# Second attention layer: the value products of four of twelve key tiles as three rounded passes

## The reference

```python
q = (hidden_states @ Wq).reshape(B, Sq, H, D)          # 16 heads of 128
k = (encoder_hidden_states @ Wk).reshape(B, Skv, H, D)
v = (encoder_hidden_states @ Wv).reshape(B, Skv, H, D)
q = rmsnorm(q, gq)
k = rmsnorm(k, gk)
scores = jnp.einsum('bqhd,bkhd->bhqk', q, k) * scale
attn = jax.nn.softmax(scores, axis=-1)
out = jnp.einsum('bhqk,bkhd->bqhd', attn, v)
return out.reshape(B, Sq, H * D) @ Wo
```

## Time and profile before

| | |
|---|---|
| median of 3 runs | 2175.83 us (2175.75 to 2176.48) |
| the profiled execution | 2174.4 us, its span 2172.6 us |
| TensorE busy | 2110.9 us (97%) |
| VectorE busy | 1575.4 us (73%) |
| GpSimd busy | 1409.9 us (65%) |
| ScalarE busy | 972.9 us (45%) |
| mean granted clock of TensorE | 0.998 |

### The profile page before, as it was taken

How to read it: one execution, slowest core, us unless ns; L and a number is a source line. 1 busy time by engine, 2 the same in 40 slices (tenths; PEclk the granted TensorE clock), 3 DMA queues, 4 the chain that set the end, 5 groups by cost and what they waited for, 6 DMA issues and landing times. The chain is left out here.

```text
span 2172.6 us, 27566 instructions
## 1 busy us (share of the span) xinstructions
PE 2110.9 (97%) x8962; PEld 1571.2 (72%) x8962; DVE 1575.4 (73%) x2592; ACT 972.9 (45%) x2593; POOL 1409.9 (65%) x1120
## 2 busy tenths in 40 slices
PE   7999999999999999999999988999999999999999
PEld 7777777777777777777777556666666666665998
DVE  4889888898889888988896642556665666652677
ACT  3444445545454445444545337544444344431432
POOL 1468776887778777877787237187878787771221
PEclk9999999999999999999999999999999999999999
DMA  3000000000000000000001410011011111101110
GB/s 132 29 15 16 29 29 15 21 23 29 15 29 15 29 19 25 15 29 29 15 10 40 140 46 1 29 43 57 29 57 30 56 49 37 43 1 52 37 52 25
DMA packets 15136, 75.63 MB, mean 35 GB/s; under 512 B 1746, under 2 KB 2114, under 8 KB 13986
## 3 DMA queue, kind: packets, MB, share of 16 engines
q1 hardware_dynamic: 14994, 73.89, 10.4%
HBM read 72.97 MB, written 0.92 MB: 34 GB/s over the span
## 5 line engine op out<-in xcount | busy, mean ns | idle before, releaser
L612 POOL TENSOR_TENSOR l_prod<-l_prod 125x256 f32<-125x256 f32 x576 | 417.4, 738 | 270.4 <-DVE l_prod L677 269.7
L677 DVE TENSOR_TENSOR l_prod<-l_side,xq 125x512 f32<-125x512 f32 x576 | 394.9, 686 | 56.2 <-PE l_side L809 48.3
L954 POOL TENSOR_TENSOR l_acc<-l_acc,l_probs 125x896 f32<-125x896 f32 x160 | 346.0, 2162 | 81.7 <-ACT l_probs L904 66.0
L553 ACT ACTIVATE l_probs<-l_slots,mask_bias 125x448 f32<-125x448 f32 x384 | 237.8, 632 | 340.6 <-PE l_slots L748 340.5
L974 DVE TENSOR_TENSOR l_scaled<-l_slots,rk 125x896 f32<-125x896 f32 x192 | 207.0, 1085 | 197.8 <-PE l_slots L1039 197.7
L606 POOL TENSOR_TENSOR l_acc<-l_acc,l_probs 125x896 f32<-125x896 f32 x160 | 338.6, 2116 | 0.0
L535 ACT ACTIVATE l_prod_act<-l_prod_act 125x128 f32<-125x128 f32 x768 | 228.0, 298 | 235.3 <-DVE l_prod_act L677 235.3
L904 ACT ACTIVATE l_probs<-l_scaled 125x896 f32<-125x896 f32 x192 | 182.8, 952 | 320.7 <-DVE l_scaled L974 296.8
L686 DVE TENSOR_REDUCE l_msq<-l_prod 125x4 f32<-125x256 f32 x576 | 235.0, 410 | 1.7
L640 DVE SCALAR_TENSOR_TENSOR top<-l_side,mask_bias,top 125x448 f32<-125x448 f32 x330 | 223.4, 677 | 6.8 <-PE l_side L792 5.8
L1037 PE MATMUL l_slots<-l_qhi,l_clo 128*125 128x448 f32 x384 | 203.0, 529 | 1.4 <-DVE l_qlo L979 1.4
(11 more groups left out here) (258 smaller groups left out, 4487.9 us busy)
## 6 DMA issues: line engine op xcount, KB each, us to landing
land<-in_ctxT SPq DMA_DIRECT2D x32, 750.0 KB, 4.3
l_nat<-in_ctxN SPq DMA_DIRECT2D x16, 750.0 KB
post_we<-in_experts SPq DMA_DIRECT2D x20, 384.0 KB, 3.0
spare<-in_ctxN SPq DMA_DIRECT2D x8, 750.0 KB
nat<-in_ctxN SPq DMA_DIRECT2D x8, 750.0 KB
spare<-in_wo SPq DMA_DIRECT2D x2, 2048.0 KB, 8.5
spare<-in_wqT SPq DMA_DIRECT2D x4, 512.0 KB, 9.2
mid_fac<-in_factors SPq DMA_DIRECT2D x1, 2048.0 KB, 8.2
```

What stands on the lines that cost most here:

```text
L553: act.activation(P[t % NP][:, HALF * i:HALF * i + HALF], bank_of("S", t, i)[0:KT, 0:HALF], ACT.Exp, bias=m.mask_bias[:, b, t:t + 1]).then_ ...
L612: pool.tensor_tensor(buf[:, :, 0:C // 2], buf[:, :, 0:C // 2], buf[:, :, C // 2:C], ALU.add).then_inc(s.half_sum, 1)
L677: dve.tensor_tensor(to[:, :, :], bank, xt.unsqueeze(1).to_broadcast([KT, 4, C]), ALU.mult).then_inc(s.side_dve, 1)
L954: pool.tensor_tensor(acc[:, :], acc[:, :], P[t % NP][:, :], ALU.add).then_inc(s.acc, 1)
```

## The change

Tiles 2, 4, 6 and 8 of each batch (`SPLIT`) take the value product as three rounded passes instead of the full-precision product: both the natural-layout context (`nat`) and the probabilities (`P`) are split into a high part (a copy to float32r, on ScalarE) and a low part (the difference, on VectorE). The context's four tiles are split once for each batch, after step 10 of the batch before; the probabilities of each such tile on their own. The other eight tiles are as before.

```diff
+    SPLIT = [2, 4, 6, 8]
+    tiles_split = slice(2, 9, 2)
 ...
+        phi = [sb(f"phi{i}", [KT, QW], F32R) for i in range(2)]
+        plo = [sb(f"plo{i}", [KT, QW], F32R) for i in range(2)]
+        nat_hi = sb("nat_hi", [KT, len(SPLIT), C], F32R)
+        nat_lo = sb("nat_lo", [KT, len(SPLIT), C], F32R)
 ...  ScalarE
+            def probs_high(b, t):
+                at = SPLIT.index(t)
+                act.wait_ge(s.probs, NT * b + t + 1)
+                act.activation(phi[at % 2][:, :], P[t % NP][:, :], ACT.Copy).then_inc(s.p_hi, 1)
+            def values_high(b):
+                need(act, (s.ld_nat0, s.ld_nat1)[b % 2], 8 * (b + b % 2))
+                need(act, s.pv, NT * (b - 1) + SPLIT[-1] + 1 if b > 0 else 0)
+                act.activation(nat_hi[:, :, :], nat[b % 2][:, tiles_split, :], ACT.Copy).then_inc(s.nat_hi, 1)
 ...
                     for bt, tt in tile_ahead(LAG, b, t):
                         exp(bt, bt % 2, tt)
+                        if tt in SPLIT:
+                            probs_high(bt, tt)
+                    if t == SPLIT[-1] + 2 and nxt:
+                        values_high(b + 1)
 ...
             high_parts(0, 0)
+            values_high(0)
 ...  VectorE
+            def probs_low(b, t):
+                at = SPLIT.index(t)
+                dve.wait_ge(s.p_hi, len(SPLIT) * b + at + 1)
+                dve.tensor_tensor(plo[at % 2][:, :], P[t % NP][:, :], phi[at % 2][:, :].bitcast(F32), ALU.subtract).then_inc(s.p_lo, 1)
+            def values_low(b):
+                dve.wait_ge(s.nat_hi, b + 1)
+                dve.tensor_tensor(nat_lo[:, :, :], nat[b % 2][:, tiles_split, :], nat_hi[:, :, :].bitcast(F32),
+                                  ALU.subtract).then_inc(s.nat_lo, 1)
 ...
                     for bt, tt in tile_ahead(LAG, b, t):
                         scale_scores(bt, bt % 2, tt)
+                    if t + 1 in SPLIT:
+                        probs_low(b, t + 1)
+                    if t == SPLIT[-1] + 2 and nxt:
+                        values_low(b + 1)
                     if t == 0 and not start:
                         invert(b - 1)
 ...
             query_low(0, 0)
+            values_low(0)
 ...  TensorE, values_half
-                last = pe.matmul(psO[:, half, 0:HALF], nat[par][:, t, :], P[t % NP][:, cols], start=t == 0, stop=t == NT - 1)
+                if t in SPLIT:
+                    at = SPLIT.index(t)
+                    pe.wait_ge(s.nat_lo, b + 1)
+                    pe.wait_ge(s.p_lo, len(SPLIT) * b + at + 1)
+                    pe.matmul(psO[:, half, 0:HALF], nat_lo[:, at, :], phi[at % 2][:, cols], start=False, stop=False)
+                    pe.matmul(psO[:, half, 0:HALF], nat_hi[:, at, :], plo[at % 2][:, cols], start=False, stop=False)
+                    last = pe.matmul(psO[:, half, 0:HALF], nat_hi[:, at, :], phi[at % 2][:, cols], start=False, stop=False)
+                else:
+                    last = pe.matmul(psO[:, half, 0:HALF], nat[par][:, t, :], P[t % NP][:, cols], start=t == 0, stop=t == NT - 1)
```

More of the change, by code:

```diff
@@ L841, in second_attention @@
     s = semaphores(sem, tag, [
-        "ld_land", "ld_nat0", "ld_nat1", "ctx_hi", "ctx_lo", "q_hi", "q_lo", "scores", "scaled", "probs", "pv", "acc",
+        "ld_land", "ld_nat0", "ld_nat1", "ctx_hi", "ctx_lo", "q_hi", "q_lo", "scores", "scaled", "nat_hi", "nat_lo", "probs", "p_hi", "p_lo", "pv", "acc",
         "den", "inv", "o_raw", "o_done", "fold_pe", "fold_act", "fold_dve", "y_pe", "y_act"])
     LAG, NP = 2, 3
+    SPLIT = [2, 4, 6, 8]
+    tiles_split = slice(2, 9, 2)
     with ExitStack() as ctx:
```

## The result

The kernel after takes 2284.59 us (median of 4 runs, 2283.86 to 2285.12) against 2175.79 before: ratio 1.0501, 95% interval 1.0484 to 1.0517. Slower, as forecast, and 20 us over the 2265 predicted, inside the range of 2222 to 2300. The profiled execution has a span of 2283.2 us, 110.6 more than before.

A forecast was written before the change was run, and what follows sets the result against it. TensorE, without slack in `second_attention`, was taken to bound the kernel. Waits of 6.9 us less 1.1 saved, carried as +5.9 a batch, over fifteen batches 89 us, made 2174.4 into 2263, as a median 2265; range 2222 to 2300.

The forecast's parts named there:

- What comes off: TensorE's value products of four tiles in 16 batches: 0.28 us saved a tile, 17.9 us, called the whole gain.
- The walk: One batch followed through all engines' queues: 34.29 us becomes 40.2, +5.9 a batch, 89 us over fifteen batches.
- the faster rival: All engines in `second_attention`: everything added lies in slack, `probs_low(2)` is done by 8.2 us; 2158 us; chance 0.03.
- The port: VectorE and GpSimd exclude one another by whole instructions: a subtraction costs 1.09 us with GpSimd idle, up to 3.1 otherwise.
- Step 1, end of the batch before: Values of tile 0: TensorE waits 1.87 us for ScalarE's copy, as `values_low` waits for GpSimd's long instruction.
- Step 2, tile 2: Values of tile 2: TensorE waits 1.34 us for `probs_low(2)`, behind the reciprocals and scale 3 on VectorE.
- Step 3, tile 4: Values of tile 4: GpSimd's addition goes between the halves of `normalise`, `probs_low(4)` is late; TensorE waits 3.0 us.
- Step 4, tiles 6 and 8: Values of tiles 6 and 8: TensorE loses 0.04 and 0.66 us to `probs_low`; `query_low` delays the scale of tile 9.
- order at the port: VectorE's `normalise` keeps its second half ahead of GpSimd's addition; a batch is 2.0 us shorter, 2235 us; chance 0.20.
- the clock falls in the waits: TensorE's clock falls in tile 4's 3.0 us wait: 2.6 a batch, 39 more at most, up to 2304; chance 0.12.
- The first batch: No reciprocals or `normalise` ahead: some 0.5 us at tiles 4 and 8 against 0.28 saved each, about 0.
- Cheaper waits: Port costs less, `values_low` precedes GpSimd's long instruction: order alone, at least +1.3 a batch; 2195 to 2220; chance 0.07.

The follow-up runs named there:

- its twin with the clock kept up by force: The kernel after with 13 extra rounded passes on TensorE just before its wait for the low part of tile 4; 2265.61 us (1.041).
- The third experiment: The kernel after with `normalise` as one instruction of 896 columns in place of two of 448; 2238.31 us (1.0281).
- The splitting alone: The kernel after with TensorE taking all tiles in full precision, while the other engines still split; 2247.74 us (1.0329).
- the first experiment: The kernel after without splitting: TensorE's rounded passes for the four tiles take operands that are ready anyway; 2162.24 us (0.9935).

## Why the prediction held, and by what it was off

*What comes off,* 17.9 us: 13.6 measured with ready operands. The saving of tile 2 lies ahead of the one place where VectorE sets the time, which the first part of the prediction had named, and is absorbed there. The walk had that in it (it runs over VectorE's queue), the sum of "the whole gain" and the price of the faster rival, 2158, had not.

*The port,* "by whole instructions": right. `probs_low` took 1.07 at tile 2, where GpSimd is idle, and 2.09 at tile 4, as forecast; at tile 6, forecast at 2 or more, it took 1.08, since the addition was over by then.

*Step 1, end of the batch before,* 1.87: measured 1.79, from ready to start as the walk counts. *Step 2, tile 2,* 1.34: 1.22. *Step 3, tile 4,* 3.0: 2.94. *Step 4, tiles 6 and 8,* 0.04 and 0.66: 0 and 0.67. Each wait is where it was put, and the first pass after each takes 0.07 longer. That is 6.9 in all, as forecast, and less 1.1 and 0.1 it makes the 5.7 that a batch grew. The forecast's own terms make 5.7 too; the 5.9 that it carried on, to 40.2 a batch and 89 us, is 0.2 over their sum. The clock's price can be read between two rows above: 12.63 - 11.09 = 1.54 us. The batch in which the clock held is 40.02 against the walk's 40.2; its twin with the clock kept up by force 40.05.

*The rival "order at the port"* (0.20) fell. It was decided by one row of another kind of instruction, and that row was the right one: 3.07 for the two halves. The third experiment, in which the gap between them is taken away, ended at 2238 where that rival had put its own kernel at 2235.

*The rival "the clock falls in the waits"* (0.12) came true on top of the forecast, and this is the step that failed: the forecast had "a granted clock of 1.0" and put the clock at nothing. I read the earlier trace rows as if it took a wait of 3.39 us; a wait of 2.75 to 2.79 was enough in 12 of 13 batches. The trace of before has a second wait of that length, between the two layers, which the forecast doesn't use, and behind it the clock held (its row, and the stretch in the columns of the earlier trace rows):

```profile
1288.50 0.47 PE L1393 MATMUL mid_bk<-mid_sql,mid_one_r 128*128 128x448 f32 x1 [3.14 <-POOL mid_sql L1236]
...
1288.00:1292.00 4.00, 3.24 (x18) 2.58 (x18) 0.62 (x1) 1.54 (x4) 3.20 (x5) 1.00 0.00 0
```

With one fall and one hold at waits near the forecast's own 3.0, an even chance would have been right. Its size was off the other way: 1.5 in most batches, since only some nine passes ran slow, and 2.6 in the two where the clock stayed down twice as long.

*The first batch,* "about 0": its denominator comes at 1445.25 against 1442.81, 2.4 late. Its four split tiles wait 0.1, 0.3, 1.0 and 1.0 us from ready to start, the first pass after each takes 0.07 longer, and the stage starts 0.9 later (the term of 0 to 1), less 1.1 saved. "Some 0.5 us at tiles 4 and 8" was 0.3 and 1.0, and the 1.0 at tile 6 was left out.

The account of the span, all from the denominators: 14 batches at 40.02 - 34.34 = 5.7 are 79.5, and the last one 5.0 (38.68 against 33.64): 84.5, forecast 89. The first batch 2.4, forecast 0. All fifteen distances together grew by 106.7, 22.2 more. Of that 19.9 are the clock in 12 batches, forecast 0. The other 2.3 are the second batch (42.36), and not the fall at tile 4: with the passes put into that wait it is 42.32 all the same. Its wait at tile 0 is 3.85, as GpSimd's long instruction begins 1.4 us ahead of the denominator there and not 3.7, and the clock falls behind that wait in both kernels; what that fall costs isn't measured apart. Behind the last denominator 1.5. Sum 110.6. The last batch shows again that a fall can be free: the clock fell there behind a wait of 2.44, and it took 38.68 against 38.70 with the clock held.

*"Cheaper waits"* had its bound right though its case did not occur: at least 1.3 a batch by order alone, and 1.5 with the additions gone (with part of the wait behind the long instruction still in it).

What wasn't seen ahead is how the three engines' loop closes. I took the waits one by one, as delays of TensorE. The splitting alone costs 72 us with TensorE waiting for none of its results, and one wait taken away (`values_low` later) returned at the next tile. A walk finds the period because it carries all queues along; its single terms don't add up when one of them is removed.

## What to carry to other kernels

Where one engine is solid, as here, moving its work to engines with 70% busy time is priced not by their idle share but by the tightest spot in the period, here the two reciprocals, and by what shares a port with what: put a subtraction of two SBUF operands where GpSimd is idle, or let GpSimd's instruction wait for it. Two back-to-back VectorE instructions on SBUF leave GpSimd a gap to step into; one instruction doesn't. And a wait on TensorE that lies near one after which the clock has been seen to fall should be priced with the fall, unless another wait stands close behind it and takes the slow passes in.

## What the runs showed of the hardware that I had not expected

- A wait added to GpSimd made the kernel 15.5 us faster, as it changed only who comes first at the port.
- TensorE's granted clock fell behind waits of 2.75 to 2.79 us in 12 batches of 13, and behind waits as short as 2.32 us (the last batch without tile 2's split); it held behind some of 2.44 us, and behind 3.29 us in three batches of the splitting alone. Behind the wait of 3.14 to 3.17 us between the layers, which all 14 kernels have, it fell in five profiled executions and held in nine. So between 2.3 and 3.3 us the length of the wait alone doesn't settle it. Where no wait was over 1.8 us it held in every plain batch. Thirteen passes that nobody needs, put into the wait, kept it at 2.4 GHz and made the kernel 19 us faster.
- What had been expected, and the first experiment bore out (0.84 for three tiles): a value product of a tile in full precision and one in three rounded passes differ by 0.28 us and no more on TensorE (0.376 x 4 against 0.204 x 6), while making the operands of one takes ScalarE 0.95 and VectorE mostly 1.07 to 2.1 us.
